# Decoder layer with sorted experts: two groups of three batches instead of three of two, and products of constants at the start of a batch

## What is computed

```
x = layernorm(x + attention(x))          # 8 heads, latent keys; each query sees its last 64 keys
                                         # and the 32 best of the others, found by an index score
x = layernorm(x + retention(x, ctx))     # 16 heads of 8, decay 1-gamma, causal, no softmax
probs = softmax(x @ gate_w.T); topk_probs, topk_idx = top_k(probs, 2)
hidden = relu(einsum('td,edf->tef', x, w1) + b1)      # 8 experts, 128 -> 512
all_out = einsum('tef,efd->ted', hidden, w2) + b2     # 512 -> 128
x = layernorm(x + sum over the two chosen experts of prob * all_out)
```

## Time and profile before

| what | value |
|---|---|
| median of 3 runs | 673.25 us (670.14 to 674.44) |
| the profiled execution, its own time | 671.91 us |
| its span, first to last instruction | 670.1 us |
| mean granted TensorE clock | 0.919 |
| busy: PE, DVE, ACT, POOL | 569.7, 433.0, 407.6, 265.1 us |

### The profile page before, as it was taken

The page is one execution under the profiler, slowest core; times in us unless marked ns, Lnnn a source line. Parts: engine busy times, 40 slices in busy tenths (PEclk is TensorE's granted clock), DMA queues, the critical chain, the costliest instruction groups (busy, mean ns, idle before and its releaser), DMA issues.

```text
span 670.1 us, 22002 instructions
## 1 busy us (share of the span) xinstructions
PE 569.7 (85%) x8149; PEld 437.9 (65%) x8149; DVE 433.0 (65%) x1618; ACT 407.6 (61%) x1381; POOL 265.1 (40%) x428
## 2 busy tenths in 40 slices
PE   5378987896898679989997897979995999789996
PEld 4154764574566457866787566757785667678886
DVE  0947647965885797568755894668657676434653
ACT  4446666674776567658774675568765556545352
POOL 1414901931380388016601698317502663104310
PEclk9757797998899789979997799889999899999999
DMA  5030144114013151553344143543353534785551
GB/s 169 2 123 18 22 142 177 22 26 125 13 27 115 31 158 30 172 177 104 105 148 128 49 144 86 180 134 108 108 162 105 160 95 134 221 244 187 177 159 43
DMA packets 58593, 75.84 MB, mean 113 GB/s; under 512 B 14256, under 2 KB 47480, under 8 KB 57336
## 3 DMA queue, kind: packets, MB, share of 16 engines
q1 hardware_dynamic: 56952, 71.30, 35.7%
q0 software_dynamic: 1536, 3.15, 1.6%
HBM read 58.92 MB, written 8.62 MB: 101 GB/s over the span
## 4 chain that ended last, share of the span: by engine, by line
PE 34%; POOL 10%; ACT 8%; issue 7%; DVE 6%; DMA 1%; SPq 0%; DVEq 0%; POOLq 0%; ACTq 0%
PE bW L1352 4%; PE bR L1302 4%; PE bH L1287 3%; PE bG L1075 3%; POOL gb L851 3%; PE bM L919 3%; ACT qV L1555 2%; PE bH L1338 2%; PE bG L1338 2%; ACT ht L1587 2%; PE bS L1094 2%; PE bM L1122 1%; PE bM L1117 1%; POOL sorted_tokens L863 1%; PE bC L1227 1%
## 5 line engine op out<-in xcount | busy, mean ns | idle before, releaser
L1503 ACT ACTIVATE ppn<-pp,rls 128x224 f32<-128x224 f32 (+1 forms) x128 | 58.9, 460 | 33.9 <-DVE rls L1803 32.9
L1821 DVE TENSOR_TENSOR gs<-bG,rank_t 96x512 f32<-96x512 f32 x96 | 65.5, 682 | 17.9 <-PE bG L1075 15.8
L1495 ACT ACTIVATE pp<-pp,nmx 128x224 f32<-128x224 f32 x96 | 46.5, 484 | 30.2 <-DVE nmx L1814 29.3
L809 POOL TENSOR_TENSOR r<-x,cst 128x256 f32<-128x256 f32 x8 | 5.8, 724 | 141.9 <-DVE x L1848 141.9
L1075 PE MATMUL bG<-oh,kspl 128*96 128x512 f32 x160 | 60.2, 459 | 0.0
L1884 DVE TENSOR_TENSOR sm<-bC,cst 128x512 f32<-128x512 f32 x64 | 43.6, 681 | 23.7 <-PE bC L1227 23.7
L1587 ACT ACTIVATE ht<-bH,wt 128x128 f32<-128x128 f32 x156 | 44.4, 371 | 18.0 <-PE bH L1287 18.0
L1513 ACT COPY pts<-bM 128x256 f32<-128x256 f32 x96 | 35.5, 369 | 29.1 <-PE bM L919 28.4
L919 PE MATMUL bM<-cst,ppn 128*128 128x128 f32 (+1 forms) x224 | 49.8, 293 | 3.8 <-ACT ppn L1503 3.4
L1814 DVE CUSTOM_DVE_ANT_0 pp<-bS,cst 128x224 f32<-128x224 f32 x96 | 36.4, 379 | 25.7 <-PE bS L1094 25.5
L1302 PE MATMUL bR<-wt,ht 128*128 128x128 f32 x264 | 40.8, 304 | 9.4 <-DVE taken L1964 9.3
(11 more groups left out here) (294 smaller groups left out, 1604.5 us busy)
## 6 DMA issues: line engine op xcount, KB each, us to landing
wt<-in_experts SPq DMA_DIRECT2D x61, 578.0 KB, 4.1
sidx<-far_slots SPq DMA_DIRECT2D x8, 1536.0 KB, 7.0
vstk<-gs SPq DMA_DIRECT2D x96, 64.0 KB
xs<-sorted_tokens SPq DMA_DIRECT2D x45, 64.0 KB, 3.7
expert_rows<-ot SPq DMA_DIRECT2D x45, 64.0 KB, 3.6
sorted_tokens<-acc SPq DMA_DIRECT2D x9, 256.0 KB, 2.9
cst<-shape_constants SPq DMA_DIRECT2D x1, 1595.5 KB, 6.4
xn<-in_x SPq DMA_DIRECT2D x8, 128.0 KB, 3.2
```

Source lines behind the costliest of these rows:

```text
L1495: AC(pp[:, s % 2, 0:w], bS[:, 0:w] if s < T0 else pp[:, s % 2, :], ACT.Exp, scale=1.0 if s < T0 else -1.0, bias=nmx[:, s % 2:s % 2 + 1], a ...
L1503: AC(ppn[:, t % 2, 0:w], pp[:, t % 2, 0:w], ACT.Copy, scale=rls[:, t % 2:t % 2 + 1]).then_inc(s_nrm.sem, 1)
L1821: TT(gs[:, g % 2, :].rearrange("p (t j) -> p t j", j=FAR), bG[0:96, :].rearrange("p (t j) -> p t j", j=FAR), rank_t[:, :].rearrange("p (o ...
```

## The change

Two things.

1. `GROUPS` is now (0, 1, 2) and (3, 4, 5). `most_tiles` gives (2*3*256 + 8*127)//128 = 19 tiles a group, 38 in all. Buffers that were indexed by the parity of the batch (`hm`, `place`) are now indexed by the batch modulo 3; `MOST` (the length of the tile list) is 20. By the plan, group 0 is listed in step 4 and group 1 in step 7. Second products of tiles: 0 in step 3, 3 in step 4, 9 in step 5, 7 in step 6, 3 in step 7 (slots 13 to 17), and 16 in step 8, whose `END_SLOTS` are more and closer; the dense units start in slot 13 instead of 11.5. The 12 scatters of a group are issued at once. Batch 0 is collected in step 6, slot 17, batches 1 and 2 in step 7, slots 1 and 5; their sums are in step 7, slots 1, 5 and 9, the means in 4, 8 and 12, `normed` in 6, 10 and 14. Three batches are now finished between dense units; the third is collected at unit 7 and summed two units into the second dense batch.
2. `fill(2)`: two products of 512 columns, `ident` by `wide` (both constants), written to bank `bG` and read by nobody. They are issued without a wait, after `scores` of slot 0, and before `scores` of slots 1 and 2 in batches 0 to 3, of slot 2 alone in batches 4 to 7: 4 times 6 and 4 times 4, 40 products.

```
-GROUPS = tuple((b, most_tiles(b)) for b in ((0, 1), (2, 3), (4, 5)))
+GROUPS = tuple((b, most_tiles(b)) for b in ((0, 1, 2), (3, 4, 5)))
...
-MOST = 16
+MOST = 20
...
+FILLED = ((2,), (1, 2))
...
-SUM_LATE, MEAN_LATE, NORM_LATE = 3, 5, 6
-END_SLOTS = (0, 1, 2, 3, 4, 5, 6, 7, 8, 9, 9.5, 10, 11)
-DENSE_SLOTS = (11.5, 12, 13, 14, 15, 16, 17, 18, 19)
+SUM_LATE, MEAN_LATE, NORM_LATE = 4, 7, 9
+END_SLOTS = (0, 1, 2, 3, 4, 5, 6, 7, 8, 9, 9.5, 10, 10.5, 11, 11.5, 12, 12.5)
+DENSE_SLOTS = (13, 13.5, 14, 14.5, 15, 16, 17, 18, 19)
...
-            s += 2 + 2 * (n - GROUPS[g][0][0])
+            s += 2 + 4 * (n - GROUPS[g][0][0])
...
                 if e == 1:
-                    for n in late:
-                        collect(n)
+                    collect(late[0])
+                    collect(late[1])
                 if e == 4:
-                    for n in late:
-                        summed(n)
+                    summed(late[0])
+                    summed(late[1])
                 if e == 6:
                     means(late[0])
                 if e == 7:
                     normed(late[0])
                     means(late[1])
+                    collect(late[2])
                 if e == 8:
                     normed(late[1])
...
                 if v == NE + 2:
+                    summed(late[2])
+                if v == NE + 3:
+                    means(late[2])
+                if v == NE + 4:
+                    normed(late[2])
+                if v == NE + 5:
                     dense_end(0)
...
+            wide = cst[:, cat["cos_q"][0]:cat["cos_q"][0] + 512]
+
+            def fill(products):
+
+                for _ in range(products):
+                    MM(bG[:, :], ident, wide, start=True, stop=True)
...
                 if s == int(s):
+                    if s in FILLED[i.n <= GROUPS[0][0][-1] + 1]:
+                        fill(2)
                     if s < NT:
                         scores(i, s)
                     if T0 <= s + 1 < NT:
                         gather(i, s + 1)
+                    if s == 0:
+                        fill(2)
                     return
```

More of the change, by code:

```diff
@@ L327, in build @@
         v8, i8, f8 = sb("v8", [128, NB, 2, 8]), sb("i8", [128, 2, 8], U32), sb("f8", [128, 2, 8])
-        hm, hot = sb("hm", [128, 2, 2, 2, NE]), sb("hot", [128, 2, NE], BF16)
+        hm, hot = sb("hm", [128, 3, 2, 2, NE]), sb("hot", [128, 2, NE], BF16)
         before, ones = sb("before", [128, 128], BF16), sb("ones", [128, 128], BF16)
-        taken, place = sb("taken", [128, NE]), sb("place", [128, 2, 2, NE])
+        taken, place = sb("taken", [128, NE]), sb("place", [128, 3, 2, NE])
         qq, qs, slot = sb("qq", [128, 4, NE]), sb("qs", [128, 4]), sb("slot", [128, NB, 4], U32)
@@ L1924, in router @@
                 for r in range(2):
[L1925 removed]
+                    k = od.did(TT(hm[:, i.n % 3, r, :, :], C("expert_no").rearrange("p (o e) -> p o e", o=1).broadcast_to([128, 2, NE]),
                                   f8[:, :, r:r + 1].broadcast_to([128, 2, NE]), ALU.is_equal))
                 od.wait(k)
[L1928 removed]
+                TT(hot[:, :, :], hm[:, i.n % 3, 0, :, :], hm[:, i.n % 3, 1, :, :], ALU.add).then_inc(r_m.sem, 1)
             oe = Own(dve, own_ve)
@@ L1939, in gates @@
                 for t in range(2):
-                    k = oe.did(TS(gg[:, d, t, :], hm[:, i.par, 0, t, :], v8[:, i.n, t, 0:1], None, ALU.mult))
+                    k = oe.did(TS(gg[:, d, t, :], hm[:, i.n % 3, 0, t, :], v8[:, i.n, t, 0:1], None, ALU.mult))
                 oe.wait(k)
                 for t in range(2):
-                    last = STT(gg[:, d, t, :], hm[:, i.par, 1, t, :], v8[:, i.n, t, 1:2], gg[:, d, t, :], ALU.mult, ALU.add)
+                    last = STT(gg[:, d, t, :], hm[:, i.n % 3, 1, t, :], v8[:, i.n, t, 1:2], gg[:, d, t, :], ALU.mult, ALU.add)
                 last.then_inc(r_gate.sem, 1)
@@ L1960, in stage_d @@
                     since = C("nothing") if i.n == GROUPS[GROUP_OF[i.n]][0][0] else taken[:, :]
-                    k = od.did(TT(place[:, p, :, :], bR[:, 16:32].rearrange("p (t e) -> p t e", t=2),
+                    k = od.did(TT(place[:, i.n % 3, :, :], bR[:, 16:32].rearrange("p (t e) -> p t e", t=2),
                                   since.rearrange("p (o e) -> p o e", o=1).broadcast_to([128, 2, NE]), ALU.add))
@@ L1984, in tile_list @@
                     base = row0[:, :].rearrange("p (o e) -> p o e", o=1).broadcast_to([128, 2, NE])
-                    k = os_.did(TT(place[:, b % 2, :, :], place[:, b % 2, :, :], base, ALU.add))
+                    k = os_.did(TT(place[:, b % 3, :, :], place[:, b % 3, :, :], base, ALU.add))
                     os_.wait(k)
                     k = os_.did(TT(qq[:, :, :].rearrange("p (r t) e -> p r (t e)", r=2),
-                                   hm[:, b % 2, :, :, :].rearrange("p r t e -> p r (t e)"),
-                                   place[:, b % 2, :, :].rearrange("p (o t) e -> p o (t e)", o=1).broadcast_to([128, 2, 2 * NE]), ALU.mult))
+                                   hm[:, b % 3, :, :, :].rearrange("p r t e -> p r (t e)"),
+                                   place[:, b % 3, :, :].rearrange("p (o t) e -> p o (t e)", o=1).broadcast_to([128, 2, 2 * NE]), ALU.mult))
                     os_.wait(k)
```

2 lines of the change are left out of this document (1 added, 1 removed).

## The result

The change makes the kernel slower: 677.72 us median (675.41 to 684.97) against 670.25 (665.55 to 674.44) in eight runs each, ratio 1.0131 with a 95% interval of 1.0098 to 1.0163. Two repeats beside other kernels gave 1.0143 (1.0091 to 1.0194) and 1.0177 (1.012 to 1.0234). Ratios here leave out runs more than 1.5% above the fastest of their kernel, so some differ from the quotient of the medians given with them. My 666.0 us had the wrong sign. The profiled execution took 684.97 us, the longest of the eight and 7.3 us above their median; its span is 683.2.

The account below looks back on a forecast made before the run. The prediction took TensorE's queue, broken by waits on others, to bound the kernel. From 671.9 us, regrouping alone at +0.5 and the products of constants at -6.4 gave 666.0 us, range 652 to 681.

Parts of the forecast that it names:

- (a): Step 3 loses its tiles and its scatter and becomes like batch 2: 60.3 instead of 67.1 us, -6.8.
- (b): Step 4 gets step 3's former load with 12 scatters instead of 8, delaying `kdn`: +0.6 us, bounds -4.6 and +3.
- (c): Step 5 gets step 4's load, 71.7 instead of 77.5 us: -5.8, including a 4.42 us wait of DVE.
- (d): Step 6 has 7 tiles instead of 9, two fewer at 1.5 us each: -3.0 us.
- (e): Step 7: POOL's longer queue ends the scatter later and delays SP's `vstk` loads: +7.0 us, bounds +3 and +10.
- (f): The end: four more tiles, 16 instead of 12, at 2.1 us each: +8.5 us, bounds 6.6 and 11.6.
- (g): Products of constants at batch starts raise TensorE's clock: -6.4 us in all; -6.6 in batches 1 to 3, +3.0 in batch 0.
- Rival 2: POOL's and SP's queues or the weight loads cost their upper bounds: 673.4 us, no change; chance 0.20.
- Rival 1: TensorE's clock stays up longer than counted, also in later steps: 655 us; chance 0.22.
- Rival 3: The products of constants run at the low clock and stand on the path at batch starts: 691 us; chance 0.13.
- the wait of the flip of `kdn`: Sign in batch 4: TensorE's flip of POOL's keys waits 4 to 5 us for POOL.
- the long `vstk` wait: Sign in batch 7: DVE or PE waits for the `vstk` DMA between 30 and 41 us after the batch's start.

Follow-up runs that it names:

- the later finishing: Changed kernel with collects, sums, means and normed rows of group 0 seven slots later: ratio 1.0141, again 1.0195; ten slots later 1.0203.
- The removal of three places: Kernel before with three tile places (slots 10, 13, 15) taken from step 7 and three given to the end: ratio 1.0155.

## Why the prediction was wrong

By its own steps, in us of the two pairs of traces:

| step | predicted | measured |
|---|---|---|
| (a) step 3 | -6.8 | -7.6, -8.6 |
| (b) step 4 | +0.6 (-4.6 to +3) | +1.0, +3.3 |
| (c) step 5 | -5.8 | -7.8, -7.9 |
| (d) step 6 | -3.0 | -2.5, -2.3 |
| (e) step 7 | +7.0 (+3 to +10) | +13.2, +12.5 |
| (f) end tiles | +8.5 (6.6 to 11.6) | +12.0, +10.8 |
| (g) products, all | -6.4 | 0.9977 alone: -1.6 (-3.8 to +0.8); batches 1 and 2: +0.1 to -0.6 each |

**(e)** is the step whose mechanism failed, and the largest miss: 5.5 to 6.2 us. Next in size is (g), 4.8 us short, then (f), 2.3 to 3.5.

In (e) the part that I counted was there: POOL's queue, the scatter's end, SP's `vstk` behind it. I put the collect of batch 1 between rotation and scatter, but the collect of batch 0 nowhere, since its place is in step 6. It belongs ahead of the rotation: it could not run before the last tile's rows were stored. DVE had written those rows by 480.1, but SP issued the store at 488.51, behind eight DMAs of `ckw` that begin at 483.33, 3.7 us before batch 7 starts. In the kernel before the first collect ran 42 us after the start of batch 5, with the rotation long done. DVE then began the row numbers 12.5 us after the start of batch 7 instead of 9.6 (504.73 - 492.22, 514.56 - 504.94), and had the first scatter's 3.7 us later instead of 1.5, slowed by POOL's sum. (The third batch's row numbers come behind those and did not hold the first scatter.) The scatter started 5 to 7 us later than before instead of 1.8.

The second thing that (e) lacked is where this is paid. I counted only what waits for the scatter's end, from slot 6 on. In the runs 6.3 to 7.8 us are lost by tile 4, on DVE behind POOL's rotation and sum, and the later finishing takes nearly all of that away (tile 4 16.3 us after tile 0; 15.4 and 16.2 before). Behind tile 4 another 6.9 us are lost, 4.7 in the repeat, not far from the 7 that I counted. So 7.0 was about right for the part it was made of, and that part is half of the step or less. How much of the early half is the first collect and how much the sum that slows DVE stays open.

**(f)** took 2.1 us a tile from two neighbours with nothing between them. The removal of three places measured 3.3, of which 2.7 TensorE busy. Over the whole end the four tiles more of the change cost 2.7 to 3.0 each. Two neighbours show what two products and a flip take when all inputs are there; the mean over the stretch, 2.9, which I had and set aside, was the better value. So was the 2.4 us in which I reckoned a tile can be fed: the last four tiles of the changed kernel, the ones that it has more, start 2.5 to 2.9 us apart, and there the stretch has a DMA share of 0.92 to 0.94. Two of them (PE, timeline):

```profile
604.81 1.16 PE L1306 MATMUL bG<-xt,wt 128*128 128x128 f32 x8 [0.16 <-DVE xt L2032]
...
607.47 1.13 PE L1306 MATMUL bH<-xt,wt 128*128 128x128 f32 x8 [0.50 <-issue]
```

The profile names no releaser for the second, so that the loads set this pace is likely and not shown.

**(d)** assumed 1.5 us for a tile taken from a step; in step 6 two gave 2.3 to 2.5. In step 7 the three taken from the kernel before gave nothing, in the one pair of traces.

**(g)** had the mechanism (clock 1.00 at the start of batches 1 to 3, tile 3 of scores 11.3 us after tile 0 in batch 1 instead of 12.5) but not its worth. The start of batch 1 after: scores of tiles 0 to 3 (L1103) and the products (L970), PE:

```profile
103.78 0.36 PE L1103 MATMUL bS<-kd,qall 128*128 128x96 f32 x2
103.98 1.91 PE L970 MATMUL bG<-cst 128*128 128x512 f32 x4
...
106.46 1.99 PE L970 MATMUL bG<-cst 128*128 128x512 f32 x4
108.29 0.36 PE L1103 MATMUL bS<-kd,qall 128*128 128x96 f32 x2
...
109.08 1.88 PE L970 MATMUL bG<-cst 128*128 128x512 f32 x4
110.94 0.46 PE L1103 MATMUL bS<-kd,qall 128*128 128x96 f32 x2
...
115.09 0.36 PE L1103 MATMUL bS<-kd,qall 128*128 128x96 f32 x2
```

Scores of tile 1 come 4.5 us after tile 0, where they came 3.1 after it (the same stretch before is in the earlier trace rows); tile 2 is where it was (7.2 us), and from tile 2 to 3 it takes 4.15 instead of 5.35. I had halved the whole of that work; of 2.2 us expected 1.2 came, and half of that was gone by the end of the step. Why it goes is not shown. The second pair of products, at 106.46, is not hidden: it delays tile 1 by 1.4 us, and in batch 4, which lacks that pair, tile 1 comes 2.9 us after tile 0. By tile 2 the delay is gone, so it costs nothing. The 3.0 us in batch 0 did not show in the repeats.

A row on the clock: in batch 7 after, the products at 500.42 took 3.25 us for what takes 1.9 in batch 1, so there they ran at 1.2 GHz. Of the eight batches only 0 and 7 issued any of them at the low clock (3.25 to 3.78 us a pair; 1.88 to 1.99 in the others). In batch 7 TensorE had stood for 2.7 us before them, behind `rqn`, and all kernels with groups of two ran both pairs of batch 7 at 2.4 GHz. The first pair of batch 7 took 3.67 us in this trace and 1.91 in the two repeats of the same kernel. By the Trainium skill (TensorE: Matmul & The Clock Gate, section "Part 1: The HAM clock gate") the monitor runs free and does not restart with the kernel; these two values for one pair of one kernel agree with that.

**Rivals.** Rival 2 was nearest (queues at their upper bounds), and its bounds were too low: step 7 13 instead of 10, the price of a tile 2.7 to 3.0 (3.3 in the removal) instead of 2.6. Rival 1, the clock, came true as a clock and not as time: 0.919 to 0.931 in the profiles, 0.926 to 0.943 in the medians beside each other. Rival 3, products on the path, did not come true. Of the signs I named, batch 3 (59.5 us) and the clock of 1.00 at the start of batches 1 to 3 were right. Near, but outside what I gave, were the wait of the flip of `kdn` (3.5, 1.5 and 2.4 us in three traces; I said 4 to 5), batch 5 (7.8 us shorter; 4 to 7), tile 3 of scores (11.3 us in batch 1, 10.8 in 2 and 3; 10.3) and the long `vstk` wait, which ended 45.4 us after the start (30 to 41). A step 7 of 76 us and a dense start 46.7 us into step 8 were well beyond (68 to 71, 42 to 44).

The parts do not add up exactly: 1.009 times 0.998 is 1.007, the whole 1.013 to 1.018. The single parts and the whole ran on different chips, and the changed kernel never on one of 687 us; what is left may be that, or that the products of batch 7 meet a low clock in the longer step 7. That stays open.

## What to carry to other kernels

When work is dealt out anew, follow each in-order queue past the edge of the stage: an instruction that the plan places in the stage before, and whose input is now made later, blocks what stands behind it in the next one. A transfer wait taken out of one stage tends to land in the next that shares the queue; only the span to a common later point says whether anything was won (step 7 won 5.8 us, the end lost 6.4). The price of a unit of work is safer from the mean over a stretch like the one it goes to than from its best neighbours. And a raised clock was worth less than half of TensorE's work at the low clock, which is what I had counted: 1.2 us of 2.2 at the place itself, 0.5 to 0.6 by the end of the step.

## What the runs showed of the hardware

- A DVE instruction is held up by POOL's elementwise work. `row<-upto` took 1.50 us instead of 0.17 while POOL's L891 ran to 506.75; it ended at 506.78, and `qq` took 0.60 instead of 0.19 with L892 beside it. In the two repeats L1993 took 1.54 and 1.53 instead of 0.19, again up to the end of L891. The Trainium skill (SBUF — State Buffer, section "SBUF: two separate sides") describes a port pair that some DVE instructions and GpSimd's share, held by the one that starts first for its whole instruction while the other waits. The trace agrees on the waiting, 1.3 us for an instruction of 0.17, ended 0.03 us after POOL's; on who comes first it does not, since DVE's record begins 0.40 us before POOL's (505.28, 505.68).
- On two chips TensorE, DVE and ACT paused together near the end of a row of scatters or in the collects right behind it: 2.2 to 5.5 us in step 4 and 5.7 to 7.4 in step 7 with 12 in a row, 1.0 to 2.6 us with 8. The kernel before took 687 us there. The pauses are not the whole difference: step 7 took 75.0 us in the kernel with all products and groups of two there, 63.1 with batches 1 to 7 on a chip of 670 us. The traces name no releaser ("remote", "issue"); on the chips of 670 us no wait of DVE is put down to "remote". The cause was not found.
